# Gated network of a decoder layer: three products of a 32-row tail against one product over 96 rows

## The reference

```python
y = y @ out_proj_w.T + u
zm = rmsnorm(y, post_norm_w)
mlp = jax.nn.gelu(zm @ l1_w.T) * (zm @ l2_w.T) @ l3_w.T     # 256 -> 672 -> 256
return y + mlp
```

## Time and profile before

| | |
|---|---|
| time, median of 3 executions | 2278.83 us |
| the three | 2273.16, 2278.83, 2898.13 us |
| span of the profiled execution | 2275.8 us |
| PE busy in the span | 2026.0 us (89%) |
| DVE, ACT, POOL busy | 1494.9, 1174.4, 889.2 us |

### The profile page before, as it was taken

The page is one execution under the profiler, slowest core; times in us unless marked ns, Lnnn a source line. Parts: engine busy times, 40 slices in busy tenths (PEclk is TensorE's granted clock), DMA queues, the critical chain, the costliest instruction groups (busy, mean ns, idle before and its releaser), DMA issues. The chain is left out here.

```text
span 2275.8 us, 39720 instructions
## 1 busy us (share of the span) xinstructions
PE 2026.0 (89%) x12960; PEld 1411.1 (62%) x12960; DVE 1494.9 (66%) x2701; ACT 1174.4 (52%) x2313; POOL 889.2 (39%) x1308
## 2 busy tenths in 40 slices
PE   6786959999999948999999999999999999978998
PEld 4665847888888834565556655565556655534554
DVE  6897444444444417777777777877777777734776
ACT  6774234444444422555555555555555555554554
POOL 3444625555555421343333333343333333332232
PEclk9998979999999968999999999999999999988999
DMA  3344011222212234324433344324433344011222
GB/s 112 131 137 156 2 64 48 75 74 74 74 69 70 74 93 101 78 64 101 100 85 89 67 99 106 84 69 96 100 86 92 65 99 100 25 60 47 92 74 74
DMA packets 104638, 188.04 MB, mean 83 GB/s; under 512 B 27816, under 2 KB 77992, under 8 KB 98344
## 3 DMA queue, kind: packets, MB, share of 16 engines
q1 hardware_dynamic: 104488, 186.14, 30.3%
HBM read 110.23 MB, written 58.79 MB: 74 GB/s over the span
## 5 line engine op out<-in xcount | busy, mean ns | idle before, releaser
L1704 DVE TENSOR_REDUCE at_mneg<-at_ps_s 128x1 f32<-128x384 f32 (+3 forms) x704 | 437.8, 635 | 112.8 <-PE at_ps_s L1345 112.2
L1476 ACT ACTIVATE at_pt<-at_ps_w 128x512 f32<-128x512 f32 x640 | 375.1, 596 | 242.3 <-PE at_ps_w L1356 241.9
L1559 POOL TENSOR_SCALAR_AFFINE_SELECT at_pt<-at_pt 128x256 f32<-128x256 f32 (+1 forms) x640 | 230.7, 365 | 590.5 <-ACT at_pt L1476 588.3
L1344 PE MATMUL at_ps_s<-at_ks,at_qs 96*128 96x128 bf16 (+3 forms) x1024 | 259.1, 306 | 43.6 <-DVE at_mneg L1704 30.5
L1356 PE MATMUL at_ps_w<-at_qs,at_ks 97*128 97x512 bf16 (+3 forms) x1024 | 243.4, 300 | 5.3 <-ACT at_pt L1476 4.6
L1344 PEld LDWEIGHTS at_ps_s<-at_ks,at_qs 96*128 96x128 bf16 x1024 | 87.3, 99 | 235.4 <-DVE at_mneg L1704 136.3
L879 POOL TENSOR_TENSOR ml_m_lo<-ml_m,ml_m_hi 128x512 fp32r<-128x512 f32 x96 | 135.5, 1418 | 196.2 <-ACT ml_m_hi L794 196.0
L1372 PE MATMUL at_ps_o<-at_pt,at_val 128*32 128x512 f32 (+3 forms) x2048 | 166.0, 442 | 9.2 <-POOL at_pt L1559 9.1
L1345 PE MATMUL at_ps_s<-at_mask,at_ident 128*128 128x128 bf16 (+2 forms) x704 | 173.5, 246 | 0.0
L819 ACT ACTIVATE ml_gl<-ml_ps_g 128x512 f32<-128x512 f32 x96 | 56.6, 589 | 167.1 <-PE ml_ps_u L127 163.3
L1515 POOL TENSOR_TENSOR at_parts<-at_rest,at_parts 128x512 bf16<-128x512 f32 x64 | 74.4, 1163 | 158.7 <-ACT at_parts L1457 158.7
(11 more groups left out here) (248 smaller groups left out, 5579.3 us busy)
## 6 DMA issues: line engine op xcount, KB each, us to landing
parts_d<-at_parts SPq DMA_DIRECT2D x64, 384.0 KB, 2.5
at_ks<-parts_d SPq DMA_DIRECT2D x192, 128.0 KB, 7.2
at_qs<-parts_d SPq DMA_DIRECT2D x32, 384.0 KB, 5.0
pj_xin<-in_x SPq DMA_DIRECT2D x16, 512.0 KB, 5.1
gate_d<-pj_zc SPq DMA_DIRECT2D x16, 512.0 KB, 2.6
xv_all<-pj_turned_xv SPq DMA_DIRECT2D x16, 512.0 KB, 4.0
ml_turned_y<-xv_all SPq DMA_DIRECT2D x16, 512.0 KB, 3.5
ml_x<-gate_d SPq DMA_DIRECT2D x16, 512.0 KB, 4.2
```

The costliest lines, as they stand in the source:

```text
L1344: pe.matmul(out[:, i, :], qs[par][0:ROWS, h, toks], ks[par][0:ROWS, h, 0:(qt + 1) * P], start=i == 0, stop=False)
L1476: act.activation(pt[u % RING][:], ps_w[u % 2][:], ACT.Exp, scale=SCALE).then_inc(exped, 1)
L1559: pool.affine_select(out=diag, in_=diag, compare_op=ALU.is_ge, fill=0.0, base=0, pattern=pattern, channel_multiplier=-1).then_inc(cut, 1)
L1704: dve.tensor_reduce(mneg[:, g, h0 % HG:h0 % HG + count, qt], view_score(ps_s[s % 2], qt, count), AX_X, ALU.max, negate=True).then_inc(maxe ...
```

## The change

The 32 units of k = 5 are placed three times, one under the other, in one tile `rest` of 128 rows: rows 0 to 31 (`HI`) their high half, rows 32 to 63 (`LO`) their low half, rows 64 to 95 (`HI2`) the high half again. The weights `wd[0]` have in the same rows the high half, the high half, and the low half. One matmul over 96 rows then gives the sum of the three products. To get the values into rows 32 to 63, DVE multiplies a second time with its output on those rows; ACT copies `m` into `HI2`, then rows 0 to 63 in one copy (rows 32 to 63 so hold the rounded value), and POOL subtracts in place. `m_hi` and `m_lo` have one tile less each; the two clears and their semaphore go away; two semaphores, `rest_mult` and `rest_high`, come in. In `longconv` the low half of `wd` is made for the first five tiles, and for rows 64 to 95 of the sixth in place in `wd[0]`.

```diff
 # longconv, weight_low
+                elif k == 4:
+                    low_rows = slice(2 * FR, 3 * FR)
+                    whole = slice(0, FT - 1)
+                    dve.tensor_tensor(lo[:, whole, :], raws[k][:, whole, :], hi[:, whole, :].bitcast(F32), ALU.subtract).then_inc(gw.w_low, 1)
+                    dve.tensor_tensor(hi[low_rows, FT - 1, :], raws[k][low_rows, FT - 1, :],
+                                      hi[low_rows, FT - 1, :].bitcast(F32), ALU.subtract).then_inc(gw.w_low, 1)
...
 # mlp, ACT
+            def rest_parts(b):
+
+                act.wait_ge(rest_mult, b + 1)
+                wait(act, down_ready, b)
+                act.activation(rest[HI2, :], m[(FT - 1) % 2][HI, :], ACT.Copy).then_inc(rest_high, 1)
+                act.wait_ge(prod_done, FT * (b + 1))
+                act.activation(rest[0:2 * FR, :], m[(FT - 1) % 2][0:2 * FR, :], ACT.Copy).then_inc(m_high, 1)
...
-                product_high(b, par, FT - 1)
+                rest_parts(b)
...
 # mlp, POOL
+                    else:
+                        pool.wait_ge(rest_high, b + 1)
+                        pool.wait_ge(m_low, FT * b + k)
+                        pool.tensor_tensor(rest[LO, :], m[k % 2][LO, :], rest[LO, :].bitcast(F32), ALU.subtract).then_inc(m_low, 1)
+                        pool.wait_ge(m_low, FT * (b + 1))
...
 # mlp, PE
-            pe.wait_ge(gw.w_low, 8)
-            pe.wait_ge(cleared, 2)
+            pe.wait_ge(gw.w_low, 9)
...
-                    mm = products3(pe, ps_o[:, q, :],
-                                   [(m_hi[slot(k, par)][:, toks], m_lo[slot(k, par)][:, toks]) for k in range(FT)],
-                                   [(wd[0][:, k, :], wd[1][:, k, :]) for k in range(FT)])
+                    products3(pe, ps_o[:, q, :],
+                              [(m_hi[slot(k, par)][:, toks], m_lo[slot(k, par)][:, toks]) for k in range(FT - 1)],
+                              [(wd[0][:, k, :], wd[1][:, k, :]) for k in range(FT - 1)], last=False)
+                    mm = pe.matmul(ps_o[:, q, :], rest[0:3 * FR, toks], wd[0][0:3 * FR, FT - 1, :], start=False, stop=True)
...
 # mlp, DVE
-            for tail in (m_hi[slot(FT - 1, 0)], m_lo[slot(FT - 1, 0)]):
-                dve.memset(tail[:].bitcast(F32), 0.0).then_inc(cleared, 1)
...
-                    up = ps_u[k % 2][:] if k < FT - 1 else ps_g[k % 2][FR:2 * FR, :]
-                    dve.tensor_tensor(m[k % 2][rows(k), :], gl[k % 2][rows(k), :], up, ALU.mult).then_inc(prod_done, 1)
+                    if k < FT - 1:
+                        dve.tensor_tensor(m[k % 2][:], gl[k % 2][:], ps_u[k % 2][:], ALU.mult).then_inc(prod_done, 1)
+                    else:
+                        up = ps_g[k % 2][FR:2 * FR, :]
+                        dve.tensor_tensor(m[k % 2][HI, :], gl[k % 2][HI, :], up, ALU.mult).then_inc(rest_mult, 1)
+                        dve.tensor_tensor(m[k % 2][LO, :], gl[k % 2][HI, :], up, ALU.mult).then_inc(prod_done, 1)
...
-        "w_down": tiles(np.concatenate([down, np.zeros((P - FR, D), down.dtype)])),
+        "w_down": tiles(np.concatenate([down] + [down[FW:]] * 2 + [np.zeros((P - 3 * FR, D), down.dtype)])),
```

More of the change, by code:

```diff
@@ L686, in mlp @@
         m = [n.sb(f"m{i}", [P, T]) for i in range(2)]
-        m_hi = [n.sb(f"m_hi{i}", [P, T], F32R) for i in range(FT + 2)]
-        m_lo = [n.sb(f"m_lo{i}", [P, T], F32R) for i in range(FT + 2)]
+        m_hi = [n.sb(f"m_hi{i}", [P, T], F32R) for i in range(FT + 1)]
+        m_lo = [n.sb(f"m_lo{i}", [P, T], F32R) for i in range(FT + 1)]
+        rest = n.sb("rest", [P, T], F32R)
         r = n.sb("r", [P, QT, D])
@@ L706, in mlp @@
             n.sem(s) for s in ("r_set", "stats", "aggr", "lnv_set", "lnr_set", "x1_set"))
-        cleared = n.sem("cleared")
+        rest_mult, rest_high = n.sem("rest_mult"), n.sem("rest_high")
         pool_settled, dve_settled = n.sem("pool_settled"), n.sem("dve_settled")
         block = ctx.enter_context(nc.Block())
+        HI, LO, HI2 = (slice(i * FR, (i + 1) * FR) for i in range(3))
         def slot(k, par):
@@ L793, in product_high @@
                     wait(act, down_ready, b - 1)
-                act.activation(m_hi[slot(k, par)][rows(k), :], m[k % 2][rows(k), :], ACT.Copy).then_inc(m_high, 1)
+                act.activation(m_hi[slot(k, par)][:], m[k % 2][:], ACT.Copy).then_inc(m_high, 1)
+            def rest_parts(b):
[4 more added lines that the diff above has]
+                act.activation(rest[0:2 * FR, :], m[(FT - 1) % 2][0:2 * FR, :], ACT.Copy).then_inc(m_high, 1)
             def norm(b):
@@ L878, in step @@
                     pool.wait_ge(m_high, FT * b + k + 1)
-                    pool.tensor_tensor(m_lo[slot(k, par)][rows(k), :], m[k % 2][rows(k), :],
-                                       m_hi[slot(k, par)][rows(k), :].bitcast(F32), ALU.subtract).then_inc(m_low, 1)
+                    if k < FT - 1:
+                        pool.tensor_tensor(m_lo[slot(k, par)][:], m[k % 2][:], m_hi[slot(k, par)][:].bitcast(F32),
+                                           ALU.subtract).then_inc(m_low, 1)
+                    else:
[3 more added lines that the diff above has]
+                        pool.wait_ge(m_low, FT * (b + 1))
                     if k == 0 and not is_last(b):
```

## The result

| | before | after |
|---|---|---|
| time, median of 5 executions | 2273.64 us | 2264.36 us (2262.46 to 2265.46) |
| ratio after to before | | 0.9954, 95% interval 0.9941 to 0.9967 |
| span of the profiled execution | 2275.8 us | 2260.7 us |
| DVE, ACT busy in it | 1494.9, 1174.4 us | 1504.4, 1184.1 us |

What follows compares the result with a forecast made beforehand. It took `mlp` to be bound by PE's work and the DVE/ACT/POOL relay, nearly equal chains from the end of `down`. Terms -15.1, +1.4 and +0.1 gave -13.6 us from 2275.8, so 2262 us, range 2253 to 2277.

Steps and rivals of the forecast that it cites:

- The bound: In `mlp`, PE's work and the DVE/ACT/POOL relay are chains of nearly equal length, both starting at the end of `down`.
- Rival C: In `mlp`, PE's 0.94 us per batch comes back as idle time: 2275.8 us or a little more; chance 0.05.
- Rival D: In `mlp`, PE's product waits shrink too or the last batch's clock shifts: up to 8 us more, 2254; chance 0.05.
- The matmuls: Down product: eight fewer matmuls per batch at 0.1177 us each, 15.07 us over 16 down products; 96 rows cost nothing extra.
- Rival B: Down product: each change into or out of 96 rows costs 0.11 us, 14.1 us in all, giving 2276.3; chance 0.10.
- The layernorm: ACT's layernorm starts 0.10 us later per batch behind the second copy, 1.4 us over 14 batches.
- rival A: Both products and copies run strictly in sequence, 1.31 us per batch, 18.3 us over 14, giving 2279.1; chance 0.08.
- The last batch: End of `mlp`: the tail's ACT copy comes some 0.6 us later, still ahead of 799.1; no cost in the sum.
- The split: Splitting the down weights `wd` in `longconv` on DVE ends 0 to 0.1 us later, once.
- The sum: Whole kernel: -15.1, +1.4 and +0.1 give -13.6 us, from the profiled span of 2275.8 to 2262.2 us.
- the relay as a whole: DVE's second product, ACT's second copy and POOL's added waits in `mlp`: +1.4 us, all of it ahead of the layernorm.

Runs made afterwards that it cites:

- matmuls_alone: Kernel before with one matmul instead of three for k = 5 in each block of the down product, relay as before; 2261.30 us, ratio to before 0.9937.
- third_copy: Changed kernel with one more ACT copy of 32 x 512, into an unread tile, ahead of the layernorm; 2271.59 us, ratio to before 0.9987.
- rest_128: Changed kernel with the `rest` matmul over all 128 rows, the last 32 cleared once; 2265.47 us, ratio to before 0.9959.
- relay_alone: Changed kernel with the `rest` matmul issued three times, so 72 matmuls per down product as before; ratio to before 1.0024, run again 1.0019.
- matmuls_product: matmuls_alone plus the second DVE product of the tail, into rows nobody reads; 2260.84 us, ratio to before 0.9928.

## Why the prediction was right

*The bound.* That `mlp`'s round is two chains of nearly one length, both starting at the end of `down`, was right: matmuls_alone shortens the distance by 0.95 us where 0.94 is taken out of PE, and third_copy lengthens it by 0.50 where 0.52 is put into the relay. Rival C (the gain turns into PE's wait) would have left the first at 28.95. Rival D (more than the sum) did not come either: PE's product waits stay at 13.5 us over 25 times.

*The matmuls.* Forecast 15.07 us; 14.3 and 15.9 us in two sets. The 96 rows cost nothing, as taken from the row of `attend`, though that was bf16. Rival B falls with rest_128. The sentence that rests on the Trainium skill (TensorE: Matmul & The Clock Gate, Part 3), on weight loads that overlap only with other row groups, does not, taken by itself, describe these rows: the load for 96 rows runs beside a matmul over 128, and the distance stays at 0.11 to 0.12 us.

*The layernorm.* Forecast 0.10 us per batch; the trace shows 0.10 us in the batch shown, and 0.06 us (mean of the first ten distances) to 0.08 us (median) for the loop in relay_alone. Here the step was right, in place and in size, so rival A is out as worked out (1.31 us) and right in its mechanism: third_copy shows what it would have done.

*The last batch.* "Still ahead of 799.1" was right for the tail's input, and yet the term was missed: 0.4 us, of which 0.19 come from DVE's shifted subtractions beside POOL (matmuls_product) and 0.17 stand as POOL's wait on itself, which the prediction put at 0.1 us and then at nothing.

*The split.* Forecast 0 to 0.1 us. PE's idle time ahead of the stage went from 11.31 to 11.44 us.

*The sum.* The stage in the two first traces gives 13.7 us, within 0.1 us of the forecast, and that is luck: 476.0 us was the better of two draws of the changed kernel, and 489.7 the longer of two of before. The second pair gives 9.3 us (488.1 against 478.8), the mean of both 11.5, and the times 10 to 11 us. So the gain was forecast some 3 us too large. The matmuls came out at their price, so the mis-sized term is the relay as a whole: +1.4 us in the forecast, and 4 to 5 us in the times of relay_alone (1.0019 and 1.0024). The traces show 1.9 us of it in the stage (490.8 in the mean against 488.9), in the loop and the last batch; for the other 2.4 to 3.6 us no trace shows a place, and it stays open. The time itself came within 2.4 us of 2262, by two errors against one another. The span that it started from, 2275.8, is as a number 2.2 us above the median time of before in that set, since it was an upper draw by more than the 1.7 us that a time has beyond its span (2262.46 against 2260.7). And the gain between the medians of that set was 9.3 us, 4.3 less than forecast.

## What to carry over

Look at which chains run from one end of a repeated unit to its next start; where two are of nearly equal length and share their first link, taking time out of that link pays in full, and work added to the other chain costs its full length as soon as the idle gap ahead of its next fixed step is used up. A gap is filled free of charge only by work whose input is already there: a second copy of 0.52 us fitted into 0.52 us, and a copy that waited for a second product did not. Of a stage whose head runs at a lower granted clock in some executions than in others, compare the loop's distance rather than the stage's ends or the spans; and before a difference of medians is looked for in traces, see whether the traced executions differ by as much.

## What was not expected of the hardware

The median distance in the loop of one kernel repeats within 0.03 us from execution to execution (28.95 and 28.94 before, 28.00 and 27.97 for the kernel of matmuls_alone), but the first part of `mlp`, where PE waits for other engines (busy for 48.4 of the 62 us from 322 us on, before), has a clock of 0.96 from 345 to 385 us in some traces and 0.92 or 0.91 in others. In the kernels with a changed relay and the short down product that is 59.9 against 62.1 to 62.3 us for the same stretch of work. The last distance, with the wait of 6.60 us for POOL in it, was 27.75 us in one trace of the kernel before and 26.49 us in the other. Times of the kernel before on one chip spread over 2272.7 to 2284.1 us, more than the effect studied.

Two DVE products in a row, the second with its output on rows 32 to 63 instead of 0 to 31, started 0.71 us apart, 0.03 us after the end of the first. The subtraction behind them in the last batch, back on rows from 0 on, starts 0.71 us after the second product as well (781.81 and 782.52). Where the rows stay, the next operation starts before the end of the one ahead: `add_x` 0.60 us after a product of 0.69 us (510.90 and 511.50 in the changed kernel), and that subtraction 0.61 us after a single product of 0.68 us (795.51 and 796.12 in the kernel before).
